# Causal mask of the first scores: from TensorE mask products to VectorE mask-and-maximum instructions

## The chip, the cores and the metric

One core of a Trainium2 chip runs a two-layer decoder as one program. The metric is the device time of the whole program in microseconds; lower is better. The profile calls the engines PE (TensorE matmul), PEld (its weight loads), DVE (VectorE), ACT (ScalarE), POOL (GpSimd) and SP (SyncE).

## The reference, cut to what matters

The input is 16 sequences of 256 rows of 256 numbers. The first layer begins with two causal attentions of 16 heads of width 16, called "latent" and "cross" in the names of the kernel; the change touches only these two. Behind them come a quantized feed-forward, a state-space block, an unmasked attention and a large feed-forward, which it leaves alone.

```
scores = einsum('bhqd,bhkd->bhqk', q, k) * scale
scores = where(k > q, -inf, scores)          # causal
attn   = softmax(scores, axis=-1)
out    = einsum('bhqk,bhkd->bhqd', attn, v) @ wo
x      = layernorm(x + out)
```

## The kernel before, in words

`piped_attention` runs one of the two attentions over the 16 sequences ("images"). Each image's scores are computed twice. The *first scores* have queries on the partitions; VectorE takes each row's maximum from them. The maxima are then split into a high and a low part, turned by TensorE, copied by ScalarE and sent by a DMA into rows of the query operand, so that the *second scores*, which have keys on the partitions, come out with the maximum already subtracted. ScalarE takes their exponentials and TensorE weighs the values with them.

An image has four groups g of four heads, each with three steps. Steps A and B: the upper 128 queries of two heads against all 256 keys, 2 x 256 columns of a PSUM bank. Step C: the lower 128 queries of four heads against the first 128 keys, 4 x 128 columns. The mask is added by TensorE: an identity matrix times a bf16 mask is written first, and the score product is accumulated on it. In the first scores that is line 442 (256 columns, steps A and B), followed by the product of line 443, and line 436 (512 columns, step C), followed by the two products of line 439. The second scores have their own mask products (lines 456 and 462) ahead of lines 459 and 464.

The first scores use two PSUM banks in turn: `query_scores` waits until the maximum two steps back has been taken (`max_taken`), and `maxima` (line 858) waits for `scored`. After the C step of groups 1 and 3, `split_maxima` (lines 864, 866) prepares eight heads' maxima, and `turn_maxima` (line 473) waits for that on TensorE.

The order of work on each engine is written out by hand in a loop over slots s. In slot s TensorE interleaves the first scores of image s+1 with the second scores of image s, and puts other products between them. Its order in a slot: A0, `turn_maxima` of half 1, the output projection of image s-2 (`project_mixed`), weighing, B0, the values projection, C0, A1, the turning of a later state (`turn_state`, line 507), B1, `turn_out` (line 573), C1, weighing, A2, `turn_maxima` of half 0 for the next image, `turn_out`, B2, a projection (queries or rope), C2, weighing, A3, `turn_mixed` (line 580), B3, a projection (keys or content), C3, and in the latent attention the latent projection, then weighing. VectorE does the maxima in the same order, and between them, in order: add the rows and take their statistics (lines 911, 914, 917) after A0; the values (881 or 883) after B0; in the latent attention the low part of queries and keys (887) after C0; the low part of the turned state (870) after A1; normalizing (898, 900) after B1; the split after C1; normalizing after A2; in the cross attention the low part of the queries (874) after B2; the low part of the mixed output (904) after A3; then a shuffle (893, latent) or the low part of the keys (874, cross) after B3; the split after C3.

In the latent attention the output projection also waits for ScalarE's latent gelu (line 697), which stands behind the exponentials of step C3, the normalizing of a state (719) and a table load.

Of the kernel before, what the change touches and what calls it, by code (L numbers as in the profile page):

```python
# [13 lines left out]
P = 128  # L14
B, S, D = 16, 256, 256
# [16 lines left out]
MASKED = -1e30  # L32
# [5 lines left out]
ALU = mybir.AluOpType  # L38
ACT = mybir.ActivationFunctionType
AX = mybir.AxisListType  # L40
# [192 lines left out]
def piped_attention(nc, core, w, ctx_dram, first):  # L233
# [3 lines left out]
    ps, ident, ident16, masks = core.ps, core.ident, core.ident16, core.masks  # L237
    scale = HD ** -0.5
    QUADS = H // 4
    HALF = PAIRS // 2  # L240
    ROWS = 3 * HD
    with ExitStack() as mem:
# [3 lines left out]
        def sem(name):  # L246
            return core.semaphore(f"{tag}_{name}")
# [101 lines left out]
        scored, max_taken, max_split, turned, ring_used = sem("scored"), sem("max_taken"), sem("max_split"), sem("turned"), sem("ring_used")  # L349
# [26 lines left out]
        def halved(b):  # L376
            return ps[:, b, :].rearrange("p (a s) -> p a s", s=S)

        def quarters(b):
            return ps[:, b, :].rearrange("p (a s) -> p a s", s=P)  # L380

        with nc.Block() as block:
# [42 lines left out]
            def _(pe):  # L425
                def query_scores(i, g, step):

                    n = 12 * i + 3 * g + "ABC".index(step)
                    if n >= 2:
                        pe.wait_ge(max_taken, n - 1)  # L430
                    if g == 0 and step == "A":
                        pe.wait_ge(stacked_in[i % 2], 128 * (i // 2) + 128)
                    b = FIRST_RING + n % 2
                    q, k = queries[i % 3], keys[i % 3]
                    if step == "C":
                        nc.tensor.matmul(quarters(b), ident16[:], masks[:, 0], start=True, stop=False, skip_group_check=True)
                        for a in range(2):
                            p = 2 * g + a
                            last = nc.tensor.matmul(quarters(b)[:, 2 * a:2 * a + 2, :], q[0:2 * ROWS, p, 0:P], k[0:2 * ROWS, p, :, 0:P], start=False, stop=True, skip_group_check=True)
                    else:  # L440
                        p = 2 * g + "AB".index(step)
                        nc.tensor.matmul(halved(b)[:, :, P:S], ident16[:], masks[:, 0, 0:2], start=True, stop=False, skip_group_check=True)
                        last = nc.tensor.matmul(halved(b), q[0:2 * ROWS, p, P:S], k[0:2 * ROWS, p], start=False, stop=True, skip_group_check=True)  # L443
                    last.then_inc(scored, 1)

                def key_scores(i, g, step):
# [145 lines left out]
                def scores(s, g, step):  # L592
                    if live(s + 1):
                        query_scores(s + 1, g, step)
                    if live(s):
                        key_scores(s, g, step)
# [251 lines left out]
            def _(dve):  # L848
                def maxima(i, g, step):
                    n = 12 * i + 3 * g + "ABC".index(step)  # L850
                    dve.wait_ge(scored, n + 1)
                    half, first = g // 2, 4 * (g % 2)
                    if step == "C":
                        out, scores = neg_max[:, half, 0, first:first + 4], quarters(FIRST_RING + n % 2)
                    else:
                        first += 2 * "AB".index(step)
                        out, scores = neg_max[:, half, 1, first:first + 2], halved(FIRST_RING + n % 2)
                    nc.vector.tensor_reduce(out, scores, AX.X, ALU.max, negate=True).then_inc(max_taken, 1)  # L858

                def split_maxima(i, half):  # L860
                    dve.drain()
# [60 lines left out]
                for s in SLOTS:  # L922
                    if live(s + 1):
                        maxima(s + 1, 0, "A")
                    if live(s - 2):
                        add_rows(s - 2)
                    if live(s + 1):
                        maxima(s + 1, 0, "B")
                    if live(s + 2):
                        copy_values(s + 2)  # L930
                    if live(s + 1):
                        maxima(s + 1, 0, "C")
# [1171 lines left out]
def decoder(nc, a, out):  # L2104

    with ExitStack() as sems, ExitStack() as mem:
        core = Core()
        core.nc, core.stage_semaphores = nc, []
        core.X = mem.enter_context(nc.sbuf_tensor("state", [P, B, TT * D], F32))
        core.ps = mem.enter_context(nc.psum_tensor("ps", [P, 8, BANK], F32))  # L2110

        def small(name, shape, dt=F32):
            return mem.enter_context(nc.sbuf_tensor(name, shape, dt))

        core.ident, core.ident16 = small("ident", [P, P]), small("ident16", [P, P], BF16)
        core.mask_f, core.masks = small("mask_f", [P, 2, P]), small("masks", [P, 2, 4, P], BF16)
        core.x_now, core.x_plus, core.rows = (small(n, [P, CHAINS * TT, D]) for n in ("x_now", "x_plus", "rows"))
        core.stats, core.moments = small("stats", [P, CHAINS * TT, 6]), small("moments", [P, CHAINS * TT, 2])
        core.shifted, core.rstd, core.minus_half, core.eps, core.minus_mean, core.offset, core.zeros = (small(n, [P, CHAINS * TT]) for n in (
            "shifted", "rstd", "minus_half", "eps", "minus_mean", "offset", "zeros"))  # L2120
        core.x_in = [sems.enter_context(nc.semaphore(f"x_in{n}")) for n in range(B // 2)]
        core.x_dram = a["x"]
        const_in = sems.enter_context(nc.semaphore("const_in"))


        with nc.Block() as block:
            @block.sync
            def _(sp):
                sp.dma_start(core.ident[:], a["c_ident"]).then_inc(const_in, 16)
                sp.dma_start(core.mask_f[:, 0, :], a["c_mask"][0]).then_inc(const_in, 16)  # L2130
                sp.dma_start(core.mask_f[:, 1, :], a["c_mask"][1]).then_inc(const_in, 16)
                for b in range(2):
                    sp.dma_start(core.X[:, b, :].rearrange("p (t d) -> p t d", d=D), a["x"][b].rearrange("(t p) d -> p t d", p=P)).then_inc(core.x_in[0], 16)

            @block.vector
            def _(dve):
                nc.vector.memset(core.eps[:], LN_EPS)
                nc.vector.memset(core.zeros[:], 0.0)
                nc.vector.memset(core.minus_half[:], -0.5)
                dve.wait_ge(const_in, 48)  # L2140
                nc.vector.tensor_copy(core.ident16[:], core.ident[:])
                for n in range(2):
                    nc.vector.tensor_copy(core.masks[:, n], core.mask_f[:, n:n + 1, :].to_broadcast([P, 4, P]))

        with ExitStack() as heads_mem:
            core.queries = [heads_mem.enter_context(nc.sbuf_tensor(f"queries{n}", [P, PAIRS, S], F32R)) for n in range(3)]
            core.keys = [heads_mem.enter_context(nc.sbuf_tensor(f"keys{n}", [P, PAIRS, 2, S], F32R)) for n in range(3)]
            core.values = [heads_mem.enter_context(nc.sbuf_tensor(f"values{n}", [P, TT, H, 2 * HD], F32)) for n in range(3)]
            core.ones_rows = nc.dram_tensor("ones_rows", [2 * H, PAIRS, 2, S], F32, kind="Internal").ap()
            piped_attention(nc, core, {k[8:]: v for k, v in a.items() if k.startswith("L0_attn")} | {k: v for k, v in a.items() if k.startswith("c_")}, None, True)  # L2150
            core.end_stage()
            piped_attention(nc, core, {k[9:]: v for k, v in a.items() if k.startswith("L0_xattn")}, a["ctx_1024"], False)
            core.end_stage()
        quantized_feed_forward(nc, core, a["L0_ffn_w_gate"], a["L0_ffn_w_up"], a["L0_ffn_w_down"])
        core.end_stage()
        state_space(nc, core, {k[8:]: v for k, v in a.items() if k.startswith("L1_attn")})
        core.end_stage()
        full_attention(nc, core, {k[9:]: v for k, v in a.items() if k.startswith("L1_xattn")}, a["ctx_1024"])
        core.end_stage()
        feed_forward(nc, core, {k[7:]: v for k, v in a.items() if k.startswith("L1_ffn")})  # L2160
        core.end_stage()
        out_done = sems.enter_context(nc.semaphore("out_done"))
        with nc.Block() as block:
            @block.sync
            def _(sp):
                for b in range(B):
                    sp.dma_start(out[b].rearrange("(t p) d -> p t d", p=P), core.X[:, b, :].rearrange("p (t d) -> p t d", d=D)).then_inc(out_done, 16)
                sp.wait_ge(out_done, 16 * B)
# [69 lines left out]
```

## Time and profile before

| | |
|---|---|
| median of 3 runs | 2272.82 us (2267.74 to 2273.52) |
| the profiled execution | 2266.7 us, span 2264.9 us |
| busy share of the span | PE 81%, PEld 67%, DVE 55%, ACT 46%, POOL 14% |
| mean granted TensorE clock | 0.908 |
| the page's chain that ended last | 13% "issue", in the last feed-forward |

The shares are means over six stages. The two head attentions take about the first 850 us of the span, and the busy shares there differ from the whole: each stage must be read by itself. The chain that ended last reaches only some 300 us back, so it says nothing on the attentions.

### The profile page before, as it was taken

How to read it: one execution, taken by the hardware profiler on the slowest of the kernel's cores; microseconds unless marked ns; L12 is line 12 of the kernel's file. 1: busy time of each engine (PE TensorE's matmuls, PEld its weight loads, DVE VectorE, ACT ScalarE, POOL GpSimd, SP SyncE). 2: the span in 40 equal slices, each digit the busy share in tenths (PEclk: the TensorE clock that was granted, in tenths of full speed). 3: DMA queues.
4: the chain of work that ended last, by engine and by line, in shares of the span. 5: the costliest groups of instructions: out<-in, count | busy, mean ns of one | idle time of the engine just before them, and what ended most of it. 6: DMA issues, size and time to landing. Idle time of an engine off the chain costs nothing. (4 is left out here: it accounts for less than half of the span.)

```text
span 2264.9 us, 34711 instructions
## 1 busy us (share of the span) xinstructions
PE 1829.9 (81%) x12518; PEld 1506.4 (67%) x12518; DVE 1247.3 (55%) x2577; ACT 1035.4 (46%) x1914; POOL 328.1 (14%) x506
## 2 busy tenths in 40 slices
PE   2799999769999985873667658838999996699996
PEld 1677777557888863552666648837887885588885
DVE  3566666446666646883677758862332222354553
ACT  1366766425555555553454435553443344422220
POOL 4443432010111103451000000000000000000000
PEclk9799999879999997996787879978999998799998
DMA  5775656067667611000000011131111113221212
GB/s 140 163 137 107 128 118 128 14 150 153 135 139 138 130 27 56 0 0 27 0 0 0 0 56 57 52 112 52 60 46 60 60 56 121 68 75 44 68 56 75
DMA packets 121121, 170.31 MB, mean 75 GB/s; under 512 B 14912, under 2 KB 88896, under 8 KB 117824
## 3 DMA queue, kind: packets, MB, share of 16 engines
q1 hardware_dynamic: 115888, 164.63, 29.1%
q10 hardware_dynamic: 5120, 4.20, 1.1%
q8 instruction: 68, 1.11, 0.2%
q14 instruction: 45, 0.37, 0.1%
HBM read 101.68 MB, written 55.05 MB: 69 GB/s over the span
## 5 line engine op out<-in xcount | busy, mean ns | idle before, releaser
L57 PE MATMUL ps<-ffn_b_gT_hi,ffn_b_h_hi 128*128 128x512 f32 x512 | 202.1, 395 | 9.5 <-DVE ffn_b_gT_lo L2077 9.5
L57 PE MATMUL ps<-ffn_a_hT_hi,ffn_a_h_hi 128*128 128x512 f32 x512 | 204.1, 399 | 2.5 <-ACT ffn_a_result L1936 2.5
L57 PE MATMUL ps<-ffn_b_gT_lo,ffn_b_h_hi 128*128 128x512 f32 x512 | 201.7, 394 | 0.0
L57 PE MATMUL ps<-ffn_a_hT_lo,ffn_a_h_hi 128*128 128x512 f32 x512 | 201.6, 394 | 0.0
L654 ACT ACTIVATE cross_probs<-ps 128x512 f32<-128x512 f32 x192 | 115.5, 603 | 132.3 <-PE ps L464 81.4
L654 ACT ACTIVATE latent_probs<-ps 128x512 f32<-128x512 f32 x192 | 115.5, 603 | 105.2 <-PE ps L464 55.4
L217 POOL TENSOR_TENSOR shifted<-moments,eps 128x4 f32<-128x4 f32 x24 | 5.3, 223 | 1091.6 <-DVE moments L188 1091.6
L858 DVE TENSOR_REDUCE latent_neg_max<-ps 128x2 f32<-128x512 f32 (+1 forms) x192 | 129.6, 681 | 48.4 <-PE ps L443 31.6
L858 DVE TENSOR_REDUCE cross_neg_max<-ps 128x2 f32<-128x512 f32 (+1 forms) x192 | 130.1, 682 | 17.1 <-PE ps L443 17.0
L1936 ACT ACTIVATE ffn_a_result<-ps,ffn_a_sh 128x512 f32<-128x512 f32 x64 | 43.2, 687 | 182.8 <-PE ps L57 182.8
L443 PE MATMUL ps<-keys,queries 96*128 96x512 f32 x256 | 124.0, 485 | 0.0
L464 PE MATMUL ps<-queries,keys 128*128 128x256 f32 x512 | 123.4, 322 | 0.0
L2057 ACT ACTIVATE ffn_b_hidden<-ps,ffn_b_sh 128x512 f32<-128x512 f32 x64 | 43.2, 688 | 174.6 <-PE ps L57 140.5
L57 PEld LDWEIGHTS ps<-ffn_b_gT_hi,ffn_b_h_hi 128*128 128x128 f32 x512 | 97.0, 190 | 30.7 <-DVE ffn_b_gT_lo L2077 9.6
L57 PEld LDWEIGHTS ps<-ffn_a_hT_hi,ffn_a_h_hi 128*128 128x128 f32 x512 | 96.3, 188 | 28.6 <-ACT ffn_a_result L1936 6.0
L57 PEld LDWEIGHTS ps<-ffn_b_gT_lo,ffn_b_h_hi 128*128 128x128 f32 x512 | 97.1, 190 | 20.9
L57 PEld LDWEIGHTS ps<-ffn_a_hT_lo,ffn_a_h_hi 128*128 128x128 f32 x512 | 96.4, 188 | 21.4
L1958 DVE SCALAR_TENSOR_TENSOR ffn_a_hidden<-ps,ffn_a_s,ffn_a_gate 128x512 f32<-128x512 f32 x64 | 48.1, 751 | 109.5 <-ACT ffn_a_gate L1924 80.7
L57 PE MATMUL ps<-ffn_a_xT_hi,ffn_a_w_hi 128*128 128x512 f32 x256 | 102.8, 402 | 2.9 <-DVE ffn_a_xT_lo L1953 2.9
L57 PE MATMUL ps<-ffn_a_xT_lo,ffn_a_w_hi 128*128 128x512 f32 x256 | 102.2, 399 | 0.0
L459 PE MATMUL ps<-queries,keys 128*128 128x128 f32 x512 | 95.4, 309 | 0.0
L1953 DVE TENSOR_TENSOR ffn_a_xT_lo<-ps,ffn_a_xT_hi 128x1024 fp32r<-128x1024 f32 x8 | 9.8, 1225 | 143.5 <-ACT ffn_a_xT_hi L1919 143.5
(415 smaller groups left out, 5486.0 us busy)
## 6 DMA issues: line engine op xcount, KB each, us to landing
ffn_between<-ffn_a_result SPq DMA_DIRECT2D x64, 256.0 KB, 2.0
ffn_b_fresh<-ffn_between SPq DMA_DIRECT2D x64, 256.0 KB, 3.2
latent_split<-latent_qk_hi SPq DMA_DIRECT2D x16, 512.0 KB, 3.6
latent_split<-latent_qk_lo SPq DMA_DIRECT2D x16, 512.0 KB, 4.5
queries<-latent_split SPq DMA_DIRECT2D x32, 256.0 KB, 4.9
keys<-latent_split SPq DMA_DIRECT2D x32, 256.0 KB, 6.7
cross_split<-cross_qk_hi SPq DMA_DIRECT2D x16, 512.0 KB, 3.0
cross_split<-cross_qk_lo SPq DMA_DIRECT2D x16, 512.0 KB, 4.1
```

The lines of the kernel that those rows point to most:

```text
L57: last = nc.tensor.matmul(out, l, r, start=start and n == 0, stop=stop and n == len(passes) - 1, **kw)
L217: nc.gpsimd.tensor_tensor(core.shifted[:, 0:tiles], core.moments[:, 0:tiles, 1], core.eps[:, 0:tiles], ALU.add)
L443: last = nc.tensor.matmul(halved(b), q[0:2 * ROWS, p, P:S], k[0:2 * ROWS, p], start=False, stop=True, skip_group_check=True)
L459: last = nc.tensor.matmul(quarters(b)[:, m, :], k[:, p, a, P:S], q[:, p, P:S], start=False, stop=True, skip_group_check=True)
L464: last = nc.tensor.matmul(halved(b)[:, a, :], k[:, p, a, 0:P], q[:, p, :], start=False, stop=True, skip_group_check=True)
L654: nc.scalar.activation(probs[:, q % 2, "ABC".index(step), :], ps[:, SECOND_RING + ring[step, i, g] % 2, :], ACT.Exp, scale=scale).then_inc ...
L858: nc.vector.tensor_reduce(out, scores, AX.X, ALU.max, negate=True).then_inc(max_taken, 1)
L1936: nc.scalar.activation(result[:, o % 2], ps[:, H1_BANK + o % 2, :], ACT.Gelu, scale=sh[:, o:o + 1]).then_inc(result_ready, 1)
L1953: nc.vector.tensor_sub(xT[1][:], ps[:, XT_BANK:XT_BANK + DT, :], f32(xT[0][:])).then_inc(xT_ready, 1)
L1958: nc.vector.scalar_tensor_tensor(hidden[:, m % 2], ps[:, UP_BANK + m % 2, :], s2[:, m:m + 1], gate[:, m % 2], ALU.mult, ALU.mult).then_inc ...
L2057: nc.scalar.activation(hidden[:, o % 2], ps[:, H2_BANK + o % 4, :], ACT.Gelu, scale=sh[:, o:o + 1]).then_inc(hidden_ready, 1)
```

## The change

The first scores get no mask product. Each score product now starts its bank, and VectorE, in place of one maximum over the bank, runs one `tensor_tensor_reduce` for each head: it adds the mask (a new f32 tile of 128 x 256, zero for the first 128 keys, the causal triangle behind), multiplies by -1, takes the minimum along the row, writes the 256 (steps A and B) or 128 (step C) masked scores back to PSUM in place, and leaves the minimum in one column of `neg_max`. The semaphore rises with the last of them. The second scores keep their mask products.

```
 if step == "C":
-    nc.tensor.matmul(quarters(b), ident16[:], masks[:, 0], start=True, stop=False, skip_group_check=True)
     for a in range(2):
         p = 2 * g + a
-        last = nc.tensor.matmul(..., start=False, stop=True, skip_group_check=True)
+        last = nc.tensor.matmul(..., start=True, stop=True, skip_group_check=True)
 else:
     p = 2 * g + "AB".index(step)
-    nc.tensor.matmul(halved(b)[:, :, P:S], ident16[:], masks[:, 0, 0:2], start=True, stop=False, skip_group_check=True)
-    last = nc.tensor.matmul(halved(b), ..., start=False, stop=True, skip_group_check=True)
+    last = nc.tensor.matmul(halved(b), ..., start=True, stop=True, skip_group_check=True)
...
-nc.vector.tensor_reduce(out, scores, AX.X, ALU.max, negate=True).then_inc(max_taken, 1)
+mask = core.causal[:, P:S] if step == "C" else core.causal[:]
+for m in range(4 if step == "C" else 2):
+    last = nc.vector.tensor_tensor_reduce(scores[:, m], scores[:, m], mask, scale=-1.0, scalar=-2 * MASKED, op0=ALU.add, op1=ALU.min, accum_out=out[:, m:m + 1])
+last.then_inc(max_taken, 1)
...
+nc.vector.memset(core.causal[:, 0:P], 0.0)
 dve.wait_ge(const_in, 48)
+nc.vector.tensor_copy(core.causal[:, P:S], core.mask_f[:, 0, :])
```

## Rows read from the trace of the kernel before

**Rows 1.** Windows of both attentions: PE, PEld, DVE, ACT, POOL busy (count), clock, DMA

```profile
102.40:417.00 314.60, 294.81 (x2730) 230.83 (x2729) 207.60 (x423) 209.91 (x399) 104.76 (x129) 1.00 0.58 115
510.00:820.00 310.00, 304.87 (x2865) 248.20 (x2867) 201.47 (x417) 167.59 (x337) 38.18 (x76) 1.00 0.65 131
```

**Rows 2.** Groups by line: the mask products that go

```profile
L442 PE MATMUL ps<-masks,ident 128*128 128x256 bf16 x256 | 72.3, 283 | 7.9 <-DMA keys<-cross_split 4.8 <-DVE cross_neg_max L858 2.0 <-DVE latent_neg_max L858 1.0
...
L436 PE MATMUL ps<-masks,ident 128*128 128x512 bf16 x128 | 49.7, 389 | 4.0 <-DVE latent_neg_max L858 3.9
```

**Rows 3.** Timeline of PE, cross attention: step A1, then `turn_state` and step B1

```profile
635.10 0.39 PE L456 MATMUL ps<-masks,ident 128*128 128x512 bf16 x1
635.14 0.74 PE L459 MATMUL ps<-queries,keys 128*128 128x128 f32 x4
635.73 0.28 PE L442 MATMUL ps<-masks,ident 128*128 128x256 bf16 x1
...
636.09 0.28 PE L462 MATMUL ps<-masks,ident 128*128 128x256 bf16 x1
...
636.45 0.60 PE L507 MATMUL ps<-ident,state 128*128 128x128 f32 x4
...
641.25 0.38 PE L473 MATMUL ps<-ident,cross_max_parts 128*16 128x128 f32 x2 [0.34 <-DVE cross_max_parts L866]
...
647.87 0.28 PE L57 MATMUL ps<-cross_cT_hi,cross_w_k_hi 128*128 128x256 f32 x1
...
652.07 0.38 PE L473 MATMUL ps<-ident,cross_max_parts 128*16 128x128 f32 x2
```

**Rows 4.** Timeline of DVE, cross attention, inside one image

```profile
638.03 0.69 DVE L870 TENSOR_TENSOR cross_xT_lo<-ps,cross_xT_hi 128x512 fp32r<-128x512 f32 x1 [1.05 <-ACT cross_xT_hi L677]
638.64 0.68 DVE L858 TENSOR_REDUCE cross_neg_max<-ps 128x2 f32<-128x512 f32 x1
639.24 0.25 DVE L898 RECIPROCAL cross_inv_sum<-ps 128x16 f32<-128x16 f32 x1
...
650.12 0.69 DVE L874 TENSOR_TENSOR cross_qk_lo<-ps,cross_qk_hi 128x512 fp32r<-128x512 f32 x1 [0.53 <-ACT cross_qk_hi L683]
...
651.75 0.18 DVE L866 TENSOR_TENSOR cross_max_parts<-cross_neg_max,cross_max_parts 128x16 fp32r<-128x16 f32 x1
...
660.13 0.69 DVE L870 TENSOR_TENSOR cross_xT_lo<-ps,cross_xT_hi 128x512 fp32r<-128x512 f32 x1 [1.05 <-ACT cross_xT_hi L677]
```

**Rows 5.** Timeline of DVE, latent attention

```profile
230.84 0.69 DVE L911 TENSOR_TENSOR rows<-ps,state 128x512 f32<-128x512 f32 x1 [2.50 <-PE ps L57]
...
253.94 0.69 DVE L911 TENSOR_TENSOR rows<-ps,state 128x512 f32<-128x512 f32 x1 [2.50 <-PE ps L57]
...
256.58 0.69 DVE L881 TENSOR_TENSOR values<-ps,latent_b_val 128x512 f32<-128x512 f32 x1 [0.21 <-PE ps L57]
...
262.89 0.17 DVE L866 TENSOR_TENSOR latent_max_parts<-latent_neg_max,latent_max_parts 128x16 fp32r<-128x16 f32 x1
```

**Rows 6.** Timeline of all engines, latent attention

```profile
240.10 0.38 PE L473 MATMUL ps<-ident,latent_max_parts 128*16 128x128 f32 x2 [0.20 <-DVE latent_max_parts L866]
...
248.76 0.60 ACT L654 ACTIVATE latent_probs<-ps 128x512 f32<-128x512 f32 x1 [1.11 <-PE ps L459]
...
252.25 0.36 PE L57 MATMUL ps<-latent_w_out_hi,latent_mixedT_hi 128*128 128x256 f32 x1 [0.95 <-ACT latent_latent_f L697]
```

**Rows 7.** Groups of DVE by line: the nearest prices

```profile
L1545 DVE SCALAR_TENSOR_TENSOR x_plus<-state,ps 128x256 f32<-128x256 f32 x32 | 12.0, 415 | 2.7 <-PE ps L57 2.6
...
L917 DVE BATCH_NORM_AGGREGATE moments<-stats 128x2 f32<-128x6 f32 x64 | 7.9, 165 | 2.7 <-issue 0.4
```

**Rows 8.** Timeline of ACT, unmasked attention: an activation with an accumulator output

```profile
1351.13 0.47 ACT L1708 ACTIVATE full_probs<-ps,full_bias 128x256 f32<-128x256 f32 x1 [1.85 <-DVE full_bias L1761]
1351.51 0.19 ACT L1708 ACTIVATION_READ_ACCUMULATOR full_probs<-ps,full_bias 128x1 f32 x1
1351.60 0.46 ACT L1708 ACTIVATE full_probs<-ps,full_bias 128x256 f32<-128x256 f32 x1
```

More of the change, by code:

```diff
@@ L435, in query_scores @@
                     if step == "C":
-                        nc.tensor.matmul(quarters(b), ident16[:], masks[:, 0], start=True, stop=False, skip_group_check=True)
                         for a in range(2):
                             p = 2 * g + a
-                            last = nc.tensor.matmul(quarters(b)[:, 2 * a:2 * a + 2, :], q[0:2 * ROWS, p, 0:P], k[0:2 * ROWS, p, :, 0:P], start=False, stop=True, skip_group_check=True)
+                            last = nc.tensor.matmul(quarters(b)[:, 2 * a:2 * a + 2, :], q[0:2 * ROWS, p, 0:P], k[0:2 * ROWS, p, :, 0:P], start=True, stop=True, skip_group_check=True)
                     else:
                         p = 2 * g + "AB".index(step)
-                        nc.tensor.matmul(halved(b)[:, :, P:S], ident16[:], masks[:, 0, 0:2], start=True, stop=False, skip_group_check=True)
-                        last = nc.tensor.matmul(halved(b), q[0:2 * ROWS, p, P:S], k[0:2 * ROWS, p], start=False, stop=True, skip_group_check=True)
+                        last = nc.tensor.matmul(halved(b), q[0:2 * ROWS, p, P:S], k[0:2 * ROWS, p], start=True, stop=True, skip_group_check=True)
                     last.then_inc(scored, 1)
@@ L2116, in decoder @@
         core.mask_f, core.masks = small("mask_f", [P, 2, P]), small("masks", [P, 2, 4, P], BF16)
+        core.causal = small("causal", [P, S])
         core.x_now, core.x_plus, core.rows = (small(n, [P, CHAINS * TT, D]) for n in ("x_now", "x_plus", "rows"))
```

## The prediction, written before the changed kernel ran

> **What bounds the kernel now.** I first read the windows by stage, since a share over the whole span mixes six stages [rows 1]. In the cross attention PE is busy for 98% of the even stretch and DVE for 65%; in the latent one PE 94%, DVE 66%, ACT 67%. The reader sees a TensorE that is nearly full, at the full clock (1.00), and a VectorE that seems to have a third of its time to spare. Read like this, the change takes from the bound and gives to the idle.
>
> A busy share doesn't say whether the spare time lies where the new work goes, so next I read the timelines of one image. The cross pattern repeats every 22.10 us (line 870 at 638.03 and 660.13 [rows 4]), the latent one every 23.10 us (line 911 at 230.84 and 253.94 [rows 5]). TensorE already waits in each cross image for the split maxima of half 0 (0.34 us at line 473 [rows 3]). In the latent attention VectorE runs from `rows` at 253.94 to the split that ends at 262.89 + 0.17 = 263.06 with one idle moment, 0.21 us ahead of the values [rows 5]; `turn_maxima` of half 0 waits for its end (0.20 us one image earlier [rows 6]), and starts at 240.10 + 23.10 = 263.20. So there are two stretches that end in `turn_maxima`, in which a longer maximum moves TensorE.
>
> **What TensorE saves.** Removed are, per image, 8 products of 256 columns and 4 of 512, in all 256 and 128 [rows 2]. At the clock of rows 1, 2.4 GHz, they stream for 0.107 and 0.213 us. That would be 8 x 0.107 + 4 x 0.213 = 1.71 us per image, 55 us over 32 images: the upper bound. (The mean durations in rows 2, 283 and 389 ns, overlap with what follows and are no saving.) But a mask product also covers the weight load of the score product behind it. The step of line 442 with its score product takes 636.09 - 635.73 = 0.36 us for 768 columns, hardly more than the 0.32 they stream, so that load is hidden now. Where products have only 128 columns the loads set the pace: lines 456 and 459 take 635.73 - 635.10 = 0.63 us, less 0.213 for the mask leaves 0.105 for each of four products that stream 0.053 [rows 3]. All A and B steps stand behind such short products (lines 459, 491, 507, 573, 580). There the load is left bare for about 0.05, and I take a saving of 0.05 per A or B step (bounds 0.05 and 0.107). C steps mostly follow 256-column products, which cover the load: 0.21.
>
> **What VectorE pays.** Now a maximum over 512 columns takes 0.60 us to the next start when something is queued behind it (638.64 to 639.24 [rows 4]). The nearest row for the new operation is line 1545, two tensors, one in PSUM, constants only, 256 columns: in pairs, so 12.0 / 16 = 0.75 per pair, less the last one's 0.415, is 0.335 from start to start [rows 7]. Between 256 and 512 columns the difference is 0.265, one column per 1.04 ns; so 128 columns cost 0.335 - 0.133 = 0.20 by an estimate from these two. No row shows VectorE giving out a minimum beside a full result. On ScalarE such an output is an instruction of its own: the read of the accumulator starts 0.38 after the activation and the next activation 0.09 later [rows 8]. VectorE's own smallest operations come in pairs, 7.9 / 32 = 0.247 per pair less 0.165, so 0.08 apart [rows 7]. I take p = 0.09 for each such read. The bounds: p = 0, if the output is free; and 0.16 (the whole 0.165) with the main operation at its full 0.415 (0.28 for 128 columns), if nothing overlaps. The write goes to PSUM, which no row shows on VectorE either; that is in the upper bound.
>
> So a step A or B costs 2 x (0.335 + p) instead of 0.60, e1 = 0.07 + 2p = 0.25 more; a step C 4 x (0.20 + p), e2 = 0.20 + 4p = 0.56 more. Per image VectorE gets 8 x 0.25 + 4 x 0.56 = 4.2 us more work for 1.2 us less on TensorE.
>
> The VectorE page of the Trainium skill ("VectorE: DVE Perf Modes", section "Two Vector instructions with no wait between them") says that an operation which also gives out its accumulator is two instructions; rows 8 agree for ScalarE. The same page's section "The DRAIN you can't avoid" says that the next operation doesn't start until the pipe is empty. By that nothing overlaps, which is the rival "no overlap" below; rows 4 speak against it for plain operations, where the record of 0.68 is followed after 0.60.
>
> **Latent, per image.** From `rows` to `turn_maxima` of half 0 stand B0, C0, A1, B1, C1 on a full VectorE: 3 e1 + 2 e2 = 1.87 more, less the 0.21 of idle ahead of the values, which goes: +1.66. The heads' low part, the turned state and the normalizing are between them and are pushed along. TensorE gets ahead and waits in `turn_maxima`, with everything queued behind it: `turn_out`, B2, the rope projection. The rest, from `turn_maxima` to the output projection at 252.25, ends in a wait for the latent gelu; ScalarE's chain to it starts at the exponential of C3 at 248.76, which waited 1.11 for TensorE [rows 6]. So B2, C2, A3, B3, C3 count there: 3 x 0.05 + 2 x 0.21 = -0.57. Half 1's split also comes later, but inside that ScalarE wait. Net +1.09 in 23.1.
>
> **Cross, per image.** Three stretches. From `turn_state` (636.45) to `turn_maxima` (641.25 [rows 3]) VectorE waits for the turned state, then runs line 870, B1, normalizing, C1, split: e1 + e2 = +0.81. From there to the second `turn_maxima` (652.07 [rows 3]) TensorE saves 0.05 + 0.21 + 0.05 + 0.05 = 0.36 up to the key projection (647.87 [rows 3]); then comes a chain: projection, ScalarE's high part, line 874 at 650.12, C3, split, which ended at 651.75 + 0.18 = 651.93, 0.14 before line 473 [rows 3, 4]. It grows by e2 = 0.56, so +0.20. The third stretch, back to `turn_state`, has slack on VectorE (1.05 idle ahead of line 870 [rows 4], less A1's 0.25 and C0's 0.56): TensorE saves B0, C0, A1, -0.31. Net +0.70 in 22.1. The cover for A0, A2, A3, B2, C2 is the time in which VectorE waits for ScalarE's high parts and for TensorE; gone, each costs its e.
>
> **Sum.** 15 slots run full in each attention: 15 x (1.09 + 0.70) = 26.9 us; the opening slots, with the same VectorE run, some 1. The second scores, the DMAs and their counts, and the later stages stay as they are; the new memset and copy run once, while constants and weights are still on their way. From the profiled 2266.7 us this gives 2294.6; that execution was 6 below the median of the runs, so on the median's footing 2300.7. I forecast between them, 2298. In general the gain or loss of a pair of images is 4 (e1 + e2) - 1.45, with e1 + e2 = 0.27 + 6p: it turns to a gain only for p below 0.015.
>
> **The rivals.**
> *Nothing overlaps* (slower still). e1 = 2 x (0.415 + 0.165) - 0.60 = 0.56, e2 = 4 x (0.28 + 0.165) - 0.60 = 1.18: 4 x 1.74 - 1.45 = 5.5 per pair, and 0.3 to 0.5 more where C0's 1.8 us makes B1 wait for its bank: +83 to +90, about 2355. With only the reads unoverlapped (p = 0.165) it is 4 x 1.26 - 1.45 = 3.6, +54, 2323. A half-rate stream with p = 0.09 adds 0.53 to each e and gives 6.0, +90. For: two f32 streams and a PSUM write that no row shows. Against: line 1545 runs at one column a cycle.
> *The output is free* (faster). One mechanism: the minimum leaves with the instruction, p = 0. Then 4 x 0.27 - 1.45 = -0.4 per pair, -6 us; if the bare loads cost nothing either, 1.92 stands for 1.45, -0.84, -13 us: 2260 to 2267. It decides from p = 0.015 (0.035 with the full saving). Against: rows 8.
> *They cancel.* TensorE's full saving of 1.92 and p = 0.05 give 4 x 0.57 - 1.92 = +0.4, +5 us; within 0.3%.
>
> **How the numbers follow.** Forecast, the overlapped pair: 0.50 (2285 to 2315). Reads or pairs dearer: 0.30 (2315 to 2360). Cancelling: 0.10. Free output: 0.10. For 8 in 10 I leave out the cheapest tenth and the dearest: 2268 to 2350. A measurement of this kernel tells 0.3% (7 us) from no change; faster 0.10, same 0.10, slower 0.80.
>
> **What the profile will show.** Right: two groups at the line of `tensor_tensor_reduce`, the operation and a read, 512 of 256 columns and 512 of 128; a pair in 0.42 and 0.29 us from start to start; periods near 24.2 (latent) and 22.8 (cross); line 473 waiting for max_parts by over 1 us per image in both; PE's busy share in cross below 98%; the later stages unchanged. Wrong: if the read isn't there, if periods fall by 0.5 or more, or if TensorE waits at the first scores for their bank in most steps, which would mean a VectorE that is full all through.

## The result, and the profile after

The changed kernel takes 2278.44 us (median of 14 runs, 2273.41 to 2284.78) where the kernel before takes 2271.65 (14 runs on the same chip): a ratio of 1.003 with a 95% interval of 1.0021 to 1.004. Two later comparisons of the same kernel gave 1.0041 (1.0028 to 1.0054) and 1.0048 (1.0034 to 1.0063). So it is slower, as forecast, but by 7 to 11 us and not by 27, and 2278.44 lies below the forecast range of 2285 to 2315.

Windows of both attentions in the changed kernel (columns as in [rows 1]):

```profile
102.40:417.00 314.60, 280.13 (x2520) 216.76 (x2547) 244.84 (x1170) 211.03 (x399) 106.36 (x130) 1.00 0.58 116
510.00:820.00 310.00, 286.56 (x2625) 232.11 (x2653) 239.47 (x1152) 166.94 (x331) 40.14 (x78) 1.00 0.67 134
```

Against [rows 1], PE fell from 94 to 89% in the latent attention and from 98 to 92% in the cross one; DVE rose from 66 to 78% and from 65 to 77%. TensorE gave up 14.7 and 18.3 us of work in these windows, and the time did not shorten.

The instructions of line 858 in the changed kernel (min/median/max duration in ns, for one operation of the line):

```profile
L858 DVE CUSTOM_DVE_ANT_0 ps<-ps,causal x1024: 286/369/468, 76.6 to 830.6; 128x128 f32<-128x128 f32 x86, 128x256 f32<-128x256 f32 x85
L858 DVE DVE_READ_ACCUMULATOR2_ANT latent_neg_max<- x512: 126/140/144, 77.0 to 423.2; 128x1 f32 x171
```

The forecast pair is there (the reads of the cross attention, another 512, are a row of their own). What it costs is read from starts, in the DVE timeline of a latent image in the changed kernel; the lines answer to [rows 5]:

```profile
256.63 0.69 DVE L912 TENSOR_TENSOR rows<-ps,state 128x512 f32<-128x512 f32 x1 [2.02 <-PE ps L57]
...
259.89 0.29 DVE L858 CUSTOM_DVE_ANT_0 ps<-ps,causal 128x128 f32<-128x128 f32 x1
260.10 0.14 DVE L858 DVE_READ_ACCUMULATOR2_ANT latent_neg_max<- 128x1 f32 x1
260.10 0.33 DVE L858 CUSTOM_DVE_ANT_0 ps<-ps,causal 128x128 f32<-128x128 f32 x1
...
260.84 1.33 DVE L888 TENSOR_TENSOR latent_qk_lo<-latent_qk_f,latent_qk_hi 128x1024 fp32r<-128x1024 f32 x1
262.10 0.42 DVE L858 CUSTOM_DVE_ANT_0 ps<-ps,causal 128x256 f32<-128x256 f32 x1
262.44 0.14 DVE L858 DVE_READ_ACCUMULATOR2_ANT latent_neg_max<- 128x1 f32 x1
262.44 0.46 DVE L858 CUSTOM_DVE_ANT_0 ps<-ps,causal 128x256 f32<-128x256 f32 x1
262.83 0.13 DVE L858 DVE_READ_ACCUMULATOR2_ANT latent_neg_max<- 128x1 f32 x1
262.83 0.68 DVE L871 TENSOR_TENSOR latent_xT_lo<-ps,latent_xT_hi 128x512 fp32r<-128x512 f32 x1
...
266.24 0.18 DVE L867 TENSOR_TENSOR latent_max_parts<-latent_neg_max,latent_max_parts 128x16 fp32r<-128x16 f32 x1
...
279.68 0.69 DVE L912 TENSOR_TENSOR rows<-ps,state 128x512 f32<-128x512 f32 x1 [2.00 <-PE ps L57]
```

Look at the equal start times. A read starts together with the next main operation and lies under it. Step A1 takes 262.83 - 262.10 = 0.73 us and step C0 260.84 - 259.89 = 0.95, where a maximum took 0.60 [rows 4]: e1 = 0.13 and e2 = 0.35 against my 0.25 and 0.56. The first main operation of each size takes 0.34 and 0.21 to the next start, which is what I had estimated (0.335 and 0.20); a read adds (0.73 / 2) - 0.335 = 0.03 and (0.95 / 4) - 0.20 = 0.04, not 0.09. The period here is 23.05 us against 23.10 before.

In the cross attention (DVE timeline, `rows` of two successive images) the period is 685.14 - 662.86 = 22.28 against 22.10:

```profile
662.86 0.69 DVE L912 TENSOR_TENSOR rows<-ps,state 128x512 f32<-128x512 f32 x1 [1.21 <-PE ps L57]
...
668.76 0.69 DVE L871 TENSOR_TENSOR cross_xT_lo<-ps,cross_xT_hi 128x512 fp32r<-128x512 f32 x1 [0.43 <-ACT cross_xT_hi L675]
```

The waits of PE in the changed kernel, its timeline at `turn_maxima` (line 471 here) and `turn_state` (line 505) in the cross attention:

```profile
661.01 0.38 PE L471 MATMUL ps<-ident,cross_max_parts 128*16 128x128 f32 x2 [0.57 <-DVE cross_max_parts L867]
...
667.18 0.60 PE L505 MATMUL ps<-ident,state 128*128 128x128 f32 x4
...
672.51 0.38 PE L471 MATMUL ps<-ident,cross_max_parts 128*16 128x128 f32 x2 [1.12 <-DVE cross_max_parts L867]
...
683.29 0.38 PE L471 MATMUL ps<-ident,cross_max_parts 128*16 128x128 f32 x2 [0.57 <-DVE cross_max_parts L867]
```

and the same in the latent attention:

```profile
263.01 0.51 PE L438 MATMUL ps<-keys,queries 96*128 96x256 f32 x2 [0.65 <-DVE latent_neg_max L858]
...
266.56 0.38 PE L471 MATMUL ps<-ident,latent_max_parts 128*16 128x128 f32 x2 [0.84 <-DVE latent_max_parts L867]
```

In the cross attention the wait at half 0 grew from 0.34 [rows 3] to 1.12, and the one at half 1 came new, 0.57 from none [rows 3]. In the latent attention it grew from 0.20 [rows 6] to 0.84. These are the stretches that the forecast named: what TensorE saves it stands waiting here. One first score per latent image also waits longer for its bank (line 438: 0.65 us in the row above; 6.5 us in ten waits from 105 to 348 us, where the kernel before had 1.7 us in ten). It is one step in twelve, and it lies in the same stretch of full VectorE.

Where the time is, from the starts of `rows` in each image's DVE timeline (us; two profiles of the kernel before, three of the changed one, means):

| | before | changed | difference |
|---|---|---|---|
| start to the first `rows` | 138.5 | 140.1 | +1.6 |
| latent, nine full images | 208.0 | 207.8 | -0.2 |
| latent, the rest | 99.4 | 99.1 | -0.3 |
| last latent to first cross `rows` | 99.2 | 102.7 | +3.5 |
| cross, eleven full images | 243.6 | 245.5 | +1.9 |
| cross, the rest | 59.0 | 59.1 | +0.1 |
| the later stages | 1419.7 | 1423.1 | +3.5 |
| span | 2267.4 | 2277.6 | +10.2 |

The even stretches, in which I had put nearly all of the loss, hold only 2 us of it. The single profiles scatter: the first `rows` come at 138.40 and 138.62 before and at 138.96, 140.25 and 141.08 in the changed kernel, and between the attentions lie 98.40 and 100.07 before and 102.26, 102.58 and 103.23 after. So the +1.6 of the start is hardly clear of the scatter, the +3.5 between the attentions is.

### The profile page after: what moved, and what is told of

It is laid out like the page before. It is cut to its first block and busy times, and to the rows that moved or that the text cites. A ratio compares the mean times of both kernels' runs of the same rounds, so it can differ in the third digit from the quotient of the medians.

```text
span 2278.9 us, 35529 instructions
## 1 busy us (share of the span) xinstructions
PE 1801.1 (79%) x12054; PEld 1481.4 (65%) x12134; DVE 1333.1 (58%) x4243; ACT 1037.4 (46%) x1914; POOL 327.8 (14%) x506
## 5 line engine op out<-in xcount | busy, mean ns | idle before, releaser
L858 DVE CUSTOM_DVE_ANT_0 ps<-ps,causal 128x256 f32<-128x256 f32 (+1 forms) x1024 | 336.0, 384 | 32.8 <-PE ps L441 21.3
L457 PEld LDWEIGHTS ps<-queries,keys 128*128 128x128 f32 x512 | 79.2, 195 | 3.4
```

The lines of the kernel that those rows point to most:

```text
L457: last = nc.tensor.matmul(quarters(b)[:, m, :], k[:, p, a, P:S], q[:, p, P:S], start=False, stop=True, skip_group_check=True)
L858: last = nc.vector.tensor_tensor_reduce(scores[:, m], scores[:, m], mask, scale=-1.0, scalar=-2 * MASKED, op0=ALU.add, op1=ALU.min, accum_ ...
```

## The experiments

The forecast's theory (call it VectorE's maxima): the time is set in stretches that end in `turn_maxima`, where the longer maxima cost more than TensorE saves elsewhere. Its rivals: the loss comes from the openings of the attentions; or one of the halves of the change is free and the other does it all.

**One half: the mask products go, the maximum stays one instruction.** This kernel leaves the causal mask out of the first scores, and its output is not the reference's.

```
-scale = HD ** -0.5
+scale = 0.01 * HD ** -0.5
...
-mask = core.causal[:, P:S] if step == "C" else core.causal[:]
-for m in range(4 if step == "C" else 2): ... tensor_tensor_reduce(...)
+nc.vector.tensor_reduce(out, scores, AX.X, ALU.max, negate=True).then_inc(max_taken, 1)
```

> Only TensorE's half of the change: the mask products of the first scores go, and VectorE takes one maximum over each bank as before, so over unmasked scores. So that no exponential vanishes with these too large maxima, the scale inside the exponentials is a hundredth of the right one; the output isn't the reference's. The re-sized sum (savings of 0.05 us per A or B step and 0.21 per C step, counted only where TensorE's order sets the end) gives -0.57 us per image in the latent body (period 22.5) and -0.67 in the cross body (21.4), about -16 us in all against the kernel before. If missing products by themselves keep TensorE at 1.2 GHz for longer in the two openings, some 5 to 7 us of that are lost again (-10 us); if the openings suffer only from VectorE's longer maxima, nothing is lost (-16 us). The upper bound, 1.71 us per image, would give -50.

Measured: 2252.9 us, 0.9921 (0.9903 to 0.9939), some 17 us faster. The periods are 22.42 (latent) and 21.34 (cross), so an image saves 0.69 and 0.76, against my terms of 0.57 and 0.36 + 0.31 = 0.67. The products stream for 55 us in all; removing them gives a third of it. TensorE's side of the sum was right.

**The other half: the products stay, VectorE does the new work.** The mask is added twice here.

```
+nc.tensor.matmul(quarters(b), ident16[:], masks[:, 0], start=True, stop=False, ...)   # step C; likewise A and B
-last = nc.tensor.matmul(..., start=True, stop=True, ...)
+last = nc.tensor.matmul(..., start=False, stop=True, ...)
```

> Only VectorE's half: the new mask-and-maximum instructions, with all mask products kept (the mask is added twice, which changes nothing). With e1 = 0.12 and e2 = 0.35 us per step, as the changed kernel's trace has them: latent body +0.5 to +0.9 us per image (the lower value if the heads' low part again takes 1.33 instead of 1.70), cross body +0.8 (period 22.9), together +17 to +22 us against the kernel before. In the openings: +1 to 2 us if the missing products are what keeps the clock low there, +6 to 8 if VectorE's longer maxima are.

Measured: 2298.84 us, 1.0123 (1.0106 to 1.014), +28 us where 17 to 22 were expected. Periods 23.79 and 23.07: +0.69 and +0.97 per image. In its profile 4.7 us of it lie between the two attentions (103.9 from the last latent to the first cross `rows` against 99.2), where the products were kept, so that loss is VectorE's. The halves add up: -0.79% and +1.23% leave +0.44%, where the whole change measured 0.30 to 0.48%. Neither is free.

**Which step costs: the new form in A and B only, and in C only.**

```
+if step == "C":        # the second kernel: if step != "C"
+    (mask product and one tensor_reduce, as before)
```

> The change in steps A and B alone; step C keeps its mask product and its one maximum. Re-sized sum with e1 = 0.13: latent 3 e1 - 0.21 - 3 x 0.05 = +0.03 us per image (as low as -0.3 if the heads' low part becomes shorter), cross e1 - 6 x 0.05 = -0.12 (the stretch to turn_maxima pays e1, the other two win). Together 0 to -4 us against the kernel before: no change or just faster. A theory by which every microsecond of VectorE work counts gives 25 images x 8 x 0.13 = +26.

> The change in step C alone; A and B keep the old form. With e2 = 0.35 and 0.21 saved per product of 512 columns: latent 2 e2 - 2 x 0.21 = +0.28 us per image, less 0.37 if C0's longer maximum pushes the heads' low part clear of GpSimd's product as in the changed kernel (-0.1); cross e2 + (e2 - 0.21) - 0.21 = +0.28. Together +2 to +7 us against the kernel before; with only_ab it should add up to the changed kernel's +7.

Measured, on one chip: A and B only 2267.88 us, 0.9991 (0.9978 to 1.0005), which can't be told from before; C only 2278.03, 1.0035 (1.0023 to 1.0047). Cross periods 21.92 and 22.48 against 22.10: -0.18 and +0.38, together +0.20 for the +0.18 of the whole. A step C takes four instructions for 512 columns, a step A or B takes two; so the 128 C steps carry the loss. The latent periods, 23.12 and 23.08, don't move with either.

**Why the latent period didn't grow.** Timeline of GpSimd and of VectorE around the heads' low part, in the kernel before:

```profile
257.13 1.28 POOL L823 TENSOR_TENSOR x_now<-x_now,latent_turned_by 128x512 f32<-128x512 f32 x1
```

```profile
257.79 1.70 DVE L887 TENSOR_TENSOR latent_qk_lo<-latent_qk_f,latent_qk_hi 128x1024 fp32r<-128x1024 f32 x1
```

and GpSimd in the changed kernel, whose VectorE line stands above (260.84, 1.33 us):

```profile
259.82 1.28 POOL L821 TENSOR_TENSOR x_now<-x_now,latent_turned_by 128x512 f32<-128x512 f32 x1
```

Both instructions read two SBUF tensors. Before, they overlap for 257.13 + 1.28 - 257.79 = 0.62 us, and VectorE's takes 1.70; after, the later start leaves 0.26 of overlap, and it takes 1.33. The longer maxima pushed it out from under GpSimd's product, which gave back 0.37 us per image. The two records less their overlaps are the same, 1.70 - 0.62 = 1.08 and 1.33 - 0.26 = 1.07: VectorE's operation ends about 1.08 after GpSimd's product has ended, as if it had waited for that end. To test this, the low part was moved behind step A1 in a kernel that is told next (the hybrid); nothing else differs:

```
-if first and live(s + 3):
-    heads_lo(s + 3)
 maxima(s + 1, 1, "A")
+if first and live(s + 3):
+    heads_lo(s + 3)
```

> The hybrid (new form only where VectorE has slack) with one more edit: in the latent attention VectorE takes the heads' low part after the maximum of A1 instead of ahead of it, so that it starts when GpSimd's product of two SBUF tensors is over. If the two share a read path and that is why it takes 1.70 us, it takes 1.22 to 1.35 here and the latent period falls from 22.42 to 22.0 to 22.1, 4 to 5 us less than the hybrid in all. If its length has another reason, nothing changes (22.42).

The low part in the latent attention (durations min/median/max in ns), without and with the move:

```profile
L901 DVE TENSOR_TENSOR latent_qk_lo<-latent_qk_f,latent_qk_hi x6: 1706/1710/1717, 208.8 to 320.9; 128x1024 fp32r<-128x1024 f32 x6
```

```profile
L901 DVE TENSOR_TENSOR latent_qk_lo<-latent_qk_f,latent_qk_hi x6: 1215/1215/1215, 208.7 to 319.7; 128x1024 fp32r<-128x1024 f32 x6
```

Where the product of GpSimd has ended, it takes 1.22, half a microsecond less than beside it, and the latent period falls from 22.42 to 22.19 (nine images 201.65 to 199.62), a little less than expected. The duration is what this kernel tests; the period may owe a part to the maximum of A1, which comes earlier. The whole time, 0.9921 (0.9906 to 0.9936), can't be told from the hybrid's 0.9925: 15 x 0.23 = 3.5 us is less than the two intervals can separate. The medians of the fourteen profiles keep to three values: 1.70 to 1.71 where C0 has its old form (before, the products alone gone, the new form in A and B only, the hybrid), 1.33 to 1.36 where C0 has the new form, 1.22 behind A1. The Trainium skill ("VectorE: DVE Perf Modes", section "Two Vector instructions with no wait between them") says that a Vector instruction with two SBUF tensors reads the second through an interface that it shares with GpSimd; these rows agree, though they don't show which interface it is. It works the other way round too. GpSimd's next operation, on two columns only, begins under the low part in the kernel before and ends 0.06 us after it; in the kernel with the move it is over before the low part starts:

```profile
258.37 1.18 POOL L793 TENSOR_TENSOR shifted<-moments,eps 128x2 f32<-128x2 f32 x1
```

```profile
252.86 0.20 POOL L801 TENSOR_TENSOR shifted<-moments,eps 128x2 f32<-128x2 f32 x1
```

It takes 1.18 us there and 0.20 here. GpSimd's records are rough, but this is the pattern of two operations that take turns, and not of two that share a rate.

**A hybrid.** Where the maxima end a stretch, the old form; elsewhere the new.

```
+def product_kept(i, g, step):
+    if (g, step) in ((1, "B"), (1, "C")):
+        return True
+    return (g, step) in ((0, "B"), (0, "C"), (1, "A")) if first else (g, step) == (3, "C")
```

> The change only in the steps whose maxima have slack on VectorE: the old form (mask product and one maximum) in B1 and C1 of both attentions, in B0, C0, A1 of the latent one and in C3 of the cross one; the new form in all others. The re-sized sum: the stretches that end in turn_maxima stay as they were, the rest loses TensorE work: latent -0.57 us per image (period 22.5), cross -0.67 (21.4), -16 us against the kernel before, less 2 to 5 for the clock in the openings. If instead VectorE's total work is what counts, it comes out between the kernel before and the changed one, within 0.3% of before.

Measured: 2252.93 us, 0.9925 (0.9912 to 0.9939), periods 22.42 and 21.35 where 22.5 and 21.4 were expected. It is 0.75% faster than the kernel before, over 1% faster than the changed one, and leaves nothing of the reference out. It reaches the time of the kernel that had no mask at all in its first scores (2252.9), as far as the intervals tell: in the steps that keep the product the product lies in time that TensorE waits anyway. This is the strongest evidence for the stretches: the map of them in the prediction chose 5 of 12 latent and 3 of 12 cross steps, and the forecast periods came within 0.1. It also speaks against a rule by amounts: with the measured 0.13 and 0.35 per step, VectorE gets 12 x 0.13 + 4 x 0.35 = 3.0 us more work per pair of images here, more than in the kernels with the new form in A and B only (16 x 0.13 = 2.1) or in C only (8 x 0.35 = 2.8), and yet it alone gains.

**The openings.** Two kernels keep the mask product for images 0 and 1 alone (`return i < 2`), with VectorE's new form everywhere; the second is the first again. A third keeps the old form wholly for these two images (product and single maximum). The changed kernel was measured twice more, and the kernel before was profiled again for the table above.

> The changed kernel, but the first scores of images 0 and 1 of both attentions keep their mask products (VectorE's new instructions everywhere; the mask added twice there). If missing products keep TensorE at 1.2 GHz in the openings, this wins back most of the 2.7 us (latent) and 4.8 us (cross) that the openings lost: -5 to -7 us against the changed kernel, and the granted clock in the openings as in the kernel before (0.73 and 0.78 in the two stretches). If VectorE's longer maxima are the cause, it stays within 1 us of the changed kernel, at +0 to +1. The bodies' periods stay at 23.07 and 22.28.

> The changed kernel once more, beside the others on the same chip, for a second profile of its two openings. If the 2.7 and 4.8 us that the openings lost in its first profile belong to the change, they are there again (first rows of the latent attention near 141, 103 us between the last rows of the latent and the first rows of the cross attention); if they are scatter of the clock and the DMAs, they differ. Time +0.2 to 0.4% against the kernel before.

> The kernel before once more, for a second profile of its openings and of the stages behind the attentions. If the openings belong to the kernel: 98.4 us between the last rows of the latent and the first of the cross attention, first rows at 138.4. What lies behind the last cross rows (1419.3 us) is the same program in all kernels: what differs there is scatter.

> The changed kernel, but images 0 and 1 of both attentions get their first scores and maxima wholly in the old form (mask product and one maximum). If the openings lose because of VectorE's longer maxima there, this wins back what the changed kernel lost outside the bodies, -4 to -5 us against it: +0.1% against the kernel before, the gap between the attentions at 98 to 99 us. If it is scatter: no difference, +0.3 to 0.4%.

> Images 0 and 1 with their mask products kept and the new instructions on VectorE, once more, beside the other two: if the products alone help in the openings, its gap is again near 100 us and its time below the changed kernel's by 3 us; if not, they agree within 1 us, as their times did the first time.

> The changed kernel, a third profile, on the same chip as the two before it: gap 102 to 103, +0.3 to 0.4% against the kernel before.

Measured: with products only, 1.0039 (1.0025 to 1.0052) and 1.0035 (1.002 to 1.005), which can't be told from the changed kernel's 1.0041 (1.0028 to 1.0054) and 1.0048 (1.0034 to 1.0063) in the two later comparisons; 99.96 and 101.87 us lie between the attentions. With the old form wholly, 2271.46 us, 1.0013 (1.0002 to 1.0023), and 98.94 us. The periods stay at 23.08 and 22.29.

The second of the kernels with products and the one with the old form differ in VectorE's maxima of four images alone. On one chip they took 2276.31 and 2271.46 us: some 5 us hang on these maxima. The changed kernel took 2279.9 us on that chip, 8 us more than the kernel with the old form. Their profiles place 4.8 of these 8 at the two openings (140.25 against 139.09 at the first `rows`, 102.58 against 98.94 between the attentions) and 2 in the later stages, whose program is the same. In the kernel of the first half, without mask products but with the old maximum, the openings are not longer than before (99.35 between the attentions). So what the change loses at the openings is mainly the longer maxima; how much of it the missing products cost lies within the noise. The kernel before, profiled again, had 100.07 where 98.4 was expected: this stretch scatters by more than 1 us, and PE's wait in it for the DMA of `keys` took 2.6 us in this profile and 7.7 in the second kernel with products.

Windows at the opening of the cross attention (columns as in [rows 1]): before,

```profile
500.00:505.00 5.00, 3.74 (x28) 3.01 (x27) 3.15 (x7) 1.80 (x4) 0.12 (x1) 1.00 0.64 210
505.00:510.00 5.00, 5.00 (x49) 3.87 (x48) 3.89 (x8) 2.87 (x5) 1.77 (x2) 1.00 0.45 105
```

changed,

```profile
500.00:505.00 5.00, 3.44 (x14) 2.85 (x14) 3.34 (x17) 0.58 (x1) 0.00 (x0) 0.50 0.70 125
505.00:510.00 5.00, 3.51 (x16) 2.54 (x15) 2.83 (x15) 1.54 (x3) 0.00 (x0) 0.50 0.36 118
```

and with the old form in images 0 and 1:

```profile
500.00:505.00 5.00, 3.69 (x27) 2.73 (x26) 2.93 (x6) 2.02 (x4) 0.00 (x0) 1.00 0.76 227
505.00:510.00 5.00, 5.00 (x45) 4.23 (x47) 3.29 (x6) 2.44 (x5) 1.89 (x2) 1.00 0.63 168
```

and with products only in images 0 and 1, the second time:

```profile
500.00:505.00 5.00, 3.32 (x23) 2.63 (x22) 3.86 (x19) 0.65 (x2) 0.00 (x0) 1.00 0.17 48
505.00:510.00 5.00, 3.26 (x26) 2.97 (x26) 3.78 (x21) 1.49 (x3) 0.61 (x1) 1.00 0.73 226
```

The last column but two is the granted clock. In the changed kernel it is 0.50 there, the lower level of 1.2 GHz, and PE gets through 30 matmuls in these 10 us where it did 77; a part of that is position, since its attention had reached this place 3.5 us later (the last latent `rows` at 448.20 and 444.68). It stands in waits like these, from its timeline:

```profile
502.61 0.79 PE L441 MATMUL ps<-keys,queries 96*128 96x512 f32 x1 [1.56 <-DVE cross_neg_max L858]
...
508.98 0.59 PE L471 MATMUL ps<-ident,cross_max_parts 128*16 128x128 f32 x2 [1.49 <-DVE cross_max_parts L867]
```

The clock isn't fixed: in the second and third profile of the changed kernel the same windows have 0.78 and 0.88, 0.84 and 0.75, while both profiles of the kernel before have 1.00. The kernel with products only has the same waits for maxima, from its timeline:

```profile
501.76 0.28 PE L448 MATMUL ps<-masks,ident 128*128 128x256 bf16 x1 [1.58 <-DVE cross_neg_max L866]
...
506.74 0.38 PE L479 MATMUL ps<-ident,cross_max_parts 128*16 128x128 f32 x2 [1.84 <-DVE cross_max_parts L875]
```

and the full clock in both windows, in both of its profiles; PE gets through 49 matmuls there (45 and 39 in the second and third profile of the changed kernel). So these waits alone don't bring the clock down, and with the full clock in these windows its whole time still can't be told from the changed kernel's: the lower clock isn't what makes most of the loss.

## Why the prediction was right in sign and wrong in size

- **The bound, and where it lies**: right. The busy shares alone would have had the change gain; the order of work in an image says that both halves of it meet at `turn_maxima`, and there PE's waits grew from 0.20 and 0.34 to 0.84 and 1.12.
- **TensorE's saving**, 0.57 and 0.67 per image: right; 0.69 and 0.76 by the kernel without mask products. The upper bound of 55 us would have been wrong by a factor of three.
- **VectorE's main operation**, 0.335 and 0.20: right; 0.34 and 0.21.
- **The read of the accumulator, p = 0.09: this is the step that failed.** The read is an instruction of its own, as I took it to be, and shows 0.14 us, but it costs only 0.03 to 0.04 from start to start, since the next main operation starts with it. I took ScalarE's spacing [rows 8] and that of small VectorE operations [rows 7], both 0.08 to 0.09. So the terms were e1 = 0.25 and e2 = 0.56 where 0.13 and 0.35 were measured. The formula of the prediction, 4 (e1 + e2) - 1.45 per pair of images, gives 4 x 0.48 - 1.45 = +0.47 with the measured costs, 7 us for 15 pairs and not 27. That this equals the measured time is partly chance: the even stretches lost 2 us, and the openings and later stages, which the formula leaves out, the rest.
- **The cross attention**: with the measured costs my terms are 0.48 + (0.35 - 0.36) - 0.31 = +0.16 per image; measured +0.18. By stretches, from [rows 3] and the PE rows of the changed kernel: `turn_state` to the turning of half 0 took 4.80 and takes 5.33 (+0.53 for 0.48), from there to the turning of half 1 10.82 and 10.78 (-0.04 for -0.01), back to `turn_state` (the rest of the period before) 6.48 and 6.17 (-0.31 for -0.31). The three stretches were right.
- **The latent attention**: the stretch from `rows` to the end of the split went from 9.12 [rows 5] to 266.24 + 0.18 - 256.63 = 9.79, +0.67. My terms give 3 x 0.13 + 2 x 0.35 - 0.21 = 0.88 with the measured costs; the low part, which I had said is only pushed along, shortened by 0.37. That leaves 0.51. Most of the other 0.16 is that B0's 0.13 is less than the idle 0.21 it falls into and so costs nothing rather than -0.08 (from `rows` to the values 2.64 before, 2.65 after), and that C1, with the split behind it, took 0.40 more and not 0.35. The rest of the period, forecast at -0.57, fell by 0.72 (13.98 to 13.26). So the net is -0.05 and not +1.09, and the even stretches of both attentions lose 2 us. Missed: that work pushed along can change its own duration, here because it leaves the company of GpSimd.
- **The openings**, forecast at "some 1": 3.5 us between the attentions, and 1.6 to the first `rows`, which is hardly clear of scatter. I had scaled the terms from the even rhythm; at the opening PE's waits for maxima lie open, and the kernel with the old form in the first two images wins the 3.5 back.
- **The later stages**, said to be unchanged: their program is the same, and they took 3.5 us more in the means. Over all profiles they scatter from 1419 to 1425 us, in kernels of either sign. What moves them stays open.
- **The rivals**: "no overlap" is refuted by the equal start times: the read lies wholly under the next operation. The Trainium skill ("VectorE: DVE Perf Modes", section "The DRAIN you can't avoid") says that an instruction waits for an empty pipe, but exempts one that isn't held, an exemption that I left out of the prediction. Here the next operation starts 0.08 before the record of the last one ends (260.10 for 260.18), so the exemption agrees. "They cancel" came nearest, for reasons of its own: it took p = 0.05, which is nearly right, and a larger saving, which isn't.

## What to carry to other kernels

Where an engine seems to have a third of its time to spare, look for the waits that end behind it before work is moved there: this change gives 0.8% back on TensorE and costs 1.2% on VectorE, and only the mix by place, new form where VectorE is waiting anyway, is faster than both. Undoing a change step by step along such a map is worth more than taking or leaving it whole.

Price an instruction by the distance between starts, in the row where another is queued behind it; a small companion instruction can cost a quarter of its recorded time. And ask of each instruction that a change delays whether it runs beside another reader of the same memory: it may get cheaper, or dearer, on the way. Here the later of the two waited for the earlier.

## What was unexpected of the hardware

- The read of VectorE's accumulator (0.14 us in the records) starts with the next main operation and adds 0.03 to 0.04 us; ScalarE's adds 0.09 [rows 8]. In the pair, the later main operation is some 0.04 longer than the first (0.46 for 0.42 us, 0.33 for 0.29).
- A VectorE operation on two SBUF tensors of 1024 columns takes 1.22 us alone, 1.33 with 0.26 us of a GpSimd product of two SBUF tensors beside it, and 1.70 with 0.62 us of it: it ends 1.07 to 1.08 us after GpSimd's product does. A GpSimd operation of two columns that starts under it shows 1.18 us in place of 0.20.
- A VectorE operation that reads and writes the same PSUM columns and adds a tile from SBUF streams them at the pace of a plain one: 256 columns in 0.34 us and 128 in 0.21 from start to start.
- At the opening of the cross attention, from 500 to 510 us, the granted clock was 0.50 in one profile of the changed kernel and 0.75 to 0.88 in the other two. It was 1.00 in the kernel before, and also in the kernel with the mask products kept there, in which PE waited up to 1.84 us at a time for maxima. What brings it down is not shown.
